# Biases as bfloat16 products in the output banks, a shorter norm chain, 60 GpSimd steps and new orders in the first and last turns of a language-model block

## The chip, the cores and the metric

The kernel runs on one core of one Trainium2 chip. The time is the device time of one launch in microseconds. PE is TensorE (its weight loads are listed as PEld), DVE is VectorE, ACT is ScalarE, POOL is GpSimd, SP is the engine that issues most of the DMAs.

## What is computed

64 sequences of 128 tokens pass through an embedding, a state-space mixer with an MLP behind it, and an 8-bit linear layer, each with a residual. Cut to what matters here:

```
h = take(quantised_table, x)                      # (64, 128, 256)
def block(x):                                     # x = layernorm(h)
    x = x + mixer(rms(x))                         # ends in  yout @ out_proj_w.T + out_proj_b
    g = gelu(rms(x) @ fc1_w.T + fc1_b)
    return x + g @ fc2_w.T + fc2_b
h = h + block(layernorm(h))
h = h + int8_linear(layernorm(h))                 # one scale from max|layernorm(h)|

mixer: z, u, B, C, dt = split(rms(x) @ in_proj_w.T); conv + silu of u, B, C
       step: z = (z + d*(u*B - A*y)) / (1 + d*d*A);  y = y + d*z;  out = y . C
       yout = (out + D_skip * u) * silu(z)
```

The biases `out_proj_b` and `fc2_b` are vectors of 256 values, the same for each token. The factor of the first norm is (var + 1e-5)^-1/2; that of the rms norm right behind it follows from the same variance.

## The kernel before

Three stages, each a block of its own. Stage 1 (to about 174 us) streams the embedding table for its maxima, gathers the 8192 rows into `h` (which stays in SBUF, tokens on partitions) and loads the weights; the last of them (`LATE_WEIGHTS`, among them both biases broadcast to 128 partitions, `out_b` and `fc2_b`) are counted on `w_late`. Stage 3 (from about 1270 us) is the 8-bit layer. Stage 2 lies between, and the change is in it.

Stage 2 takes the sequences in 16 groups of four (`G`), in turns that are software-pipelined by hand. In turn g the `first` part works on group g (input projection, convolutions, its recurrence), the `second` on group p = g-1 (scan by attention-like products, gate, output projection), the `third` on group m = g-2 (MLP), the `fourth` on group g-3 (maximum of the next norm), and `nxt` prepares the rows of group g+1. `turns` (line 1244) runs turns 0 to 3 unrolled, a loop over turns 4 to 14, and 15 to 18 unrolled; in turns 0 to 2 the later parts are missing, in turns 16 to 18 the first ones. Each engine has its own `turn` function (`pe_turn`, `act_turn`, `dve_turn`, `pool_turn`), which writes out its order; the engines meet by semaphores alone, and each executes strictly in the order written, so the order and the waits decide everything.

What the change and the prediction touch:

- `dve_quantise` (551, 554) and `dve_row_stats` (561 to 569) prepare group g+1. `pool_norm_factors` (578 to 592) makes the norm factors by a chain of nine small GpSimd operations. ACT applies them (602), PE transposes the rows (615), ACT copies them out (626), PE makes the small projections (641) and the large ones (630, 977).
- The recurrence has 64 steps of two operations. GpSimd does steps 0 to 57 (`POOL_STEPS`; 780, 782), with `pool_rms` of the group before after step 42 (`RMS_STEP`; 1117, 1119), which waits for ACT's sums of squares (1111). DVE does the last six steps (787, 789), then the keys, one reciprocal per head group (921) and the queries (927).
- PE transposes u (1001), ACT copies it to `utok` (1010), PE makes the scores of a head group (1049), DVE masks them (1060, four operations), PE makes the scan's output (1070), DVE adds the skip (1077) and gates (1084).
- `pe_out` (1095) multiplies by `w_out` into the banks `sbk`; `dve_x2` (1102) adds the layer-normed rows `xl`. Before that `dve_biases` (1025, 1027) has added `out_b` to `xl` and `fc2_b` to the rows of `h`.
- ACT sums squares (1111) and scales the rows (1128), PE transposes them (1134), ACT copies them (1141) and seeds `sbk` with the residual (1148). `pe_fc1` (1161), `act_gelu` (1171) and `pe_fc2` (1180) alternate, tile by tile, PE's down-projection three tiles behind (`LEAD`); `dve_h2` (1192) adds the banks to `h`.
- `act_x3` (1233) and `dve_max3` (1239, 1241) take the maximum of the next norm; the last group's ends stage 2.

In a full turn PE's tail of the MLP is interleaved with the scan like this (`pe_turn`, n counts tiles):

```python
for n in range(FT + LEAD):
    if third and n < FT: pe_fc1(pe, m, n, p if second else None)
    if second and n == FT:     pe_u_T(..., 0); pe_u_T(..., 1)
    if second and n == FT + 1: pe_u_T(..., 2); pe_u_T(..., 3)
    if second and n == FT + 2: pe_scores(pe, p, 0)
    if third and n >= LEAD: pe_fc2(pe, m, n - LEAD)
```

## Time and profile before

| what | value |
|---|---|
| median of 3 runs | 1327.42 us (1327.36 to 1331.47) |
| the profiled execution's own time | 1328.54 us |
| its span, first to last instruction | 1326.7 us |
| PE busy | 1124.5 us, 85% of the span |
| PE weight loads busy | 750.6 us, 57% |
| DVE busy | 1126.1 us, 85% |
| ACT busy | 791.5 us, 60% |
| POOL busy | 729.5 us, 55% |
| mean granted TensorE clock | 0.97 |

Busy time is that of instructions in execution; matmuls overlap each other's ends, so PE's counts latencies too. The granted clock is 1.00 for 2.4 GHz and 0.50 for 1.2 GHz. The profile's row of slices shows the stages: DMA at nine tenths and PE mostly below four tenths up to about 170 us, then PE at nine tenths from about 260 to 1230 us, then the last stage, in which DVE is busiest. A timeline row joins neighbouring instructions of one line on one engine: its start, its length, what it is, how many, and in brackets the idle time before it with the instruction whose end ended it.

### The profile page before, as it was taken

Reading aid. Unit: us, or ns where it says so; the run is one execution under the profiler, and the core shown is the slowest. Engines: PE = TensorE matmul, PEld = TensorE weight load, DVE = VectorE, ACT = ScalarE, POOL = GpSimd, SP = SyncE. Lnnn points to the kernel's source line nnn. Section 1 sums busy time; section 2 is a strip of 40 time slices with the busy share of each in tenths; the row PEclk is TensorE's granted clock in tenths of the full one; section 3 lists DMA queues with packets and bytes.
Section 4 is the critical chain, followed back from the end, with each engine's and each line's share of the span. In section 5 each row is a group of like instructions: output and inputs, shape, how many; then the busy total and the mean of one; then the engine's idle time right before and its main releaser. Section 6 shows DMA issues by size and latency. Waiting matters only on the chain. (4 is left out here: it accounts for less than half of the span.)

```text
span 1326.7 us, 24942 instructions
## 1 busy us (share of the span) xinstructions
PE 1124.5 (85%) x7199; PEld 750.6 (57%) x7206; DVE 1126.1 (85%) x2030; ACT 791.5 (60%) x1275; POOL 729.5 (55%) x2066
## 2 busy tenths in 40 slices
PE   2991034699999999999999999999999999997956
PEld 1550012467575766666666666576766666756534
DVE  5998969979898989898998989898989897976077
ACT  4666547383848484847475665747474848452267
POOL 8881010747485757575757575756667575730000
PEclk9999997699999999999999999999999999998879
DMA  9999801010101010101000000001010101000015
GB/s 363 407 407 419 350 11 41 1 35 2 35 1 35 1 34 1 33 4 30 10 24 15 19 18 16 18 16 28 6 34 0 34 0 35 2 18 0 0 64 190
DMA packets 37137, 91.60 MB, mean 69 GB/s; under 512 B 10141, under 2 KB 21746, under 8 KB 32738
## 3 DMA queue, kind: packets, MB, share of 16 engines
q1 hardware_dynamic: 33442, 81.32, 17.6%
q0 software_dynamic: 3072, 8.39, 1.6%
q10 hardware_dynamic: 576, 1.31, 0.3%
q8 instruction: 23, 0.38, 0.1%
q14 instruction: 24, 0.20, 0.1%
HBM read 81.29 MB, written 9.70 MB: 69 GB/s over the span
## 5 line engine op out<-in xcount | busy, mean ns | idle before, releaser
L780 POOL TENSOR_TENSOR stp<-Gs,X 128x32 f32<-128x32 f32 x870 | 263.6, 303 | 250.0 <-ACT X L753 174.9
L782 POOL TENSOR_TENSOR Gs<-Gs,stp 128x32 f32<-128x32 f32 x870 | 275.2, 316 | 68.0
L1180 PE MATMUL bank<-w_fc,gl 128*128 128x256 f32 x1024 | 244.6, 382 | 5.9 <-ACT gl L1171 5.9
L1161 PE MATMUL bank<-mT,w_fc 128*128 128x512 f32 x512 | 239.5, 601 | 1.4 <-ACT mT L1141 1.4
L1180 PEld LDWEIGHTS bank<-w_fc,gl 128*128 128x128 f32 x1024 | 189.6, 190 | 70.7 <-issue 29.7
L630 PE MATMUL bank<-xT,w_in 128*128 128x512 f32 x448 | 206.5, 601 | 0.1
L942 ACT ACTIVATE uT<-bank,cols 128x512 f32<-128x512 f32 x64 | 47.9, 774 | 229.9 <-DVE sz L1084 212.9
L1161 PEld LDWEIGHTS bank<-mT,w_fc 128*128 128x128 f32 x512 | 96.0, 192 | 87.3 <-issue 81.3
L956 DVE SCALAR_TENSOR_TENSOR uT<-bank,cols,uT 128x500 f32<-128x500 f32 (+1 forms) x192 | 133.5, 736 | 2.4
L630 PEld LDWEIGHTS bank<-xT,w_in 128*128 128x128 f32 x448 | 81.6, 191 | 83.6 <-issue 77.6
L345 DVE TENSOR_TENSOR peak<-ring,peak 128x1536 f32<-128x1536 f32 (+2 forms) x67 | 115.4, 1722 | 8.2 <-ACT ring L247 6.6
L247 ACT ACTIVATE ring<-ring 128x3072 f32<-128x3072 f32 (+4 forms) x36 | 90.8, 2531 | 49.3 <-DMA ring<-in_table 49.3
L1171 ACT ACTIVATE gl<-bank,cols 128x512 f32<-128x512 f32 x128 | 81.4, 682 | 56.9 <-PE bank L1180 49.7
L1095 PE MATMUL bank<-w_out,sz 128*128 128x256 f32 x512 | 113.9, 380 | 0.1
L1095 PEld LDWEIGHTS bank<-w_out,sz 128*128 128x128 f32 x512 | 97.3, 190 | 20.7 <-issue 7.5
L921 DVE RECIPROCAL rm<-rm 128x512 f32<-128x512 f32 x32 | 107.2, 3349 | 0.5
L753 ACT ACTIVATE X<-d_rep,cols 128x512 f32<-128x512 f32 x64 | 71.9, 1196 | 34.4 <-DMA d_rep<-d_rows 34.4
L231 POOL DMA_INDIRECT h<-in_table,ids x64 | 81.4, 1272 | 19.5 <-issue 19.2
L1060 DVE TENSOR_TENSOR MT<-bank,causal 128x512 f32<-128x512 f32 x128 | 79.3, 680 | 13.3 <-PE bank L1049 13.3
L1070 PE MATMUL bank<-MT,utok 128*64 128x128 f32 x1024 | 69.0, 286 | 24.9 <-DVE MT L1060 23.7
L1070 PEld LDWEIGHTS bank<-MT,utok 128*64 128x64 f32 x1024 | 58.1, 142 | 45.3 <-DVE MT L1060 33.0
L285 PE MATMUL bank<-ts,hot 4*128 4x256 f32 x128 | 60.4, 648 | 19.0 <-ACT hot L258 14.0
(205 smaller groups left out, 1879.2 us busy)
## 6 DMA issues: line engine op xcount, KB each, us to landing
ring<-in_table SPq DMA_DIRECT2D x31, 1536.0 KB
d_rep<-d_rows SPq DMA_DIRECT2D x128, 64.0 KB, 2.0
out<-res SPq DMA_DIRECT2D x16, 512.0 KB, 2.9
b_rep<-bc_rows SPq DMA_DIRECT2D x128, 32.0 KB, 1.8
c_rep<-bc_rows SPq DMA_DIRECT2D x128, 32.0 KB, 1.8
w_fc<-in_w_fc SPq DMA_DIRECT2D x2, 1024.0 KB, 8.5
ring<-in_table SPq DMA_DIRECT2D x2, 768.0 KB
w_in<-in_w_in ACTq DMA_DIRECT2D x1, 1088.0 KB
```

The source lines that it names most:

```text
L231: pool.indirect_dma_start(out=h[:, b * D:(b + 1) * D], out_offset=None, in_=table, in_offset=bass.IndirectOffsetOnAxis(ap=ids[:, b:b + 1], ...
L247: act.activation(ring[n % RING][0:np_, 0:nr, :], ring[n % RING][0:np_, 0:nr, :], ACT.Abs) \
L345: return dve.tensor_tensor(acc, ring[t][0:np_, r0:r0 + nr, :], acc, ALU.max)
L630: last = pe.matmul(dst, w_in[:, k, c0:c1], xT[:, k, :], start=(k == 0), stop=(k == KD - 1))
L780: pool.tensor_tensor(stp[:], Gs[:, t, ::-1, :], X2[:, t, :, :], ALU.mult).then_inc(rec.sem, 1)
L782: pool.tensor_tensor(Gs[:, t + 1, :, :], Gs[:, t, :, :], stp[:], ALU.add).then_inc(rec.sem, 1)
L921: dve.reciprocal(half_rm, half_rm).then_inc(inverted.sem, 1)
L956: dve.scalar_tensor_tensor(acc[:, :, i:], ps[:, :, 0:LEN - i], c("u_tap", f * TAPS + TAPS - 1 - i), acc[:, :, i:], ALU.mult, ALU.add).then ...
L1070: last = pe.matmul(pj[head // 2][64 * (head % 2):64 * (head % 2) + 64, j * LEN:(j + 1) * LEN], utok[:, j, head * HP:(head + 1) * HP], MT[h ...
L1095: last = pe.matmul(sbk[n][:, (j % 2) * D:(j % 2 + 1) * D], sz[:, f, j * LEN:(j + 1) * LEN], w_out[:, f, :], start=(f == 0), stop=(f == UT ...
L1161: last = pe.matmul(pj[n % 4][:, :], w_fc1[:, k, n * P:(n + 1) * P], mT[:, k, :], start=(k == 0), stop=(k == KD - 1))
L1180: last = pe.matmul(sbk[j // 2][:, (j % 2) * D:(j % 2 + 1) * D], gl[n % LEAD][:, j * LEN:(j + 1) * LEN], w_fc2[:, n, :], start=False, stop= ...
```

## The change

Four things, in stage 2.

1. **Biases on PE.** Both biases come by one DMA into `utok` (unused so far), and `dve_split_biases` makes from them a bfloat16 value, a bfloat16 remainder and a remainder of that, on partition ranges, so that three rows of `bias3` sum to the float32 value; `pick` is a 128x128 bfloat16 matrix with ones in rows 0, 64 and 96. The product `pick.T @ bias3` puts the bias on each token. `pe_bias` issues it for a whole bank (512 columns): it starts the accumulation of `pe_out`, and is added to the seeded banks ahead of the first `pe_fc2`. The DVE operations 1025 and 1027 are gone.
2. **Norm factors** by five GpSimd operations: DVE computes (1 + 1e-6) var + 1e-11 and GpSimd takes its power at once, in place of the chain of squares and products.
3. **60 GpSimd steps** in the recurrence, the rms factors after step 44, and four DVE steps.
4. **Orders.** `pe_warm` issues products whose result nobody reads: ten before turn 0, twelve in turn 1 between the transpositions, five in turn 17 ahead of the MLP's. In turn 1 DVE makes the second queries and the masks first, then quantises group 2, and takes its statistics behind the second masks. In turn 16 PE's scan pieces stand between the last down-projections, the output projection goes to the banks `tb`, ACT copies `utok` ahead of the last gelu, and DVE adds the MLP's result behind the gates. In turn 17 `act_x3` stands ahead of the gelus and `dve_max3` ahead of `dve_h2`.

```diff
-RMS_STEP = 43
-POOL_STEPS = 58
+RMS_STEP = 45
+POOL_STEPS = 60
@@ 
+        def dve_split_biases(dve):
+            whole, rest = utok[:, 0, :], utok[:, 1, :]
+            b3 = bias3[:].rearrange("p i c -> p (i c)")
+            dve.memset(pick[:], 0.0).then_inc(pick_cleared, 1)
+            dve.wait_ge(pick_cleared, 1)
+            for r in (0, 64, 96):
+                dve.memset(pick[r:r + 1, :], 1.0)
+            dve.wait_ge(bias_in, 16)
+            dve.tensor_copy(b3, whole).then_inc(halved, 1)
+            dve.wait_ge(halved, 1)
+            dve.tensor_tensor(rest[64:P], whole[64:P], b3[64:P], ALU.subtract).then_inc(halved, 1)
...
+        def pe_bias(pe, dst, i, start):
+            pe.matmul(dst[:, :].rearrange("p (j c) -> p j c", j=2), pick[:],
+                      bias3[:, i, :].unsqueeze(1).to_broadcast([P, 2, D]), start=start, stop=False,
+                      skip_group_check=True)
@@ dve_row_stats, pool_norm_factors
+            dve.tensor_scalar(lnst[:, 3, :], mv[:, :, 1], 1.0 + 1e-6, 1e-11, ALU.mult, ALU.add).then_inc(bn.sem, 1)
...
-            pool.tensor_tensor(lnst[:, 3, :], lnst[:, 2, :], lnst[:, 2, :], ALU.mult).then_inc(ln.sem, 1)
+            pool.tensor_tensor(lnst[:, 6, :], lnst[:, 3, :], half[:, 0:G], ALU.pow).then_inc(ln.sem, 1)
@@ pe_out, pe_fc2
+                pe_bias(pe, bank[n], OUT_B, True)
...
+                for i in range(2):
+                    pe_bias(pe, sbk[i], FC2_B, False)
@@ pe_turn
+        def pe_warm(pe, dst, n):
+            for _ in range(n):
+                pe.matmul(dst[:, :], ident[:], w_out[:, 0:2, :].rearrange("p f c -> p (f c)"), start=True, stop=True,
+                          skip_group_check=True)
...
+                    if last and n == FT:
+                        for j in range(G):
+                            pe_u_T(pe, p, None, j)
+                        pe_scores(pe, p, 0)
@@ dve_turn
-                if second and first and third:
-                    dve_biases(dve, p)
+                if second and not (first and third) and filling:
+                    dve_queries(dve, p, 1)
```

Where instructions moved. First PE in turn 16, from the fourth-last down-projection (1180 before, 1193 now) to the transposition of turn 17's MLP (1134, 1145). Before:

```order
L1180 MATMUL bank<-w_fc,gl 128x256 x4
L1001 MATMUL bank<-ident,uT 128x128 x8
L1180 MATMUL bank<-w_fc,gl 128x256 x4
L1001 MATMUL bank<-ident,uT 128x128 x8
L1180 MATMUL bank<-w_fc,gl 128x256 x4
L1049 MATMUL bank<-Qf,Kf 128x64 x32
L1180 MATMUL bank<-w_fc,gl 128x256 x4
L1070 MATMUL bank<-MT,utok 64x128 x16
L1049 MATMUL bank<-Qf,Kf 128x64 x32
L1070 MATMUL bank<-MT,utok 64x128 x16
L1095 MATMUL bank<-w_out,sz 128x256 x16
L1134 MATMUL bank<-ident,xr 128x128 x8
```

and now (1017 transposes u, 1057 the scores, 1078 the scan's output, 568 a bias product, 1106 the output projection, 1273 the warming products):

```order
L1193 MATMUL bank<-w_fc,gl 128x256 x4
L1017 MATMUL bank<-ident,uT 128x128 x16
L1057 MATMUL bank<-Qf,Kf 128x64 x32
L1193 MATMUL bank<-w_fc,gl 128x256 x4
L1078 MATMUL bank<-MT,utok 64x128 x16
L1057 MATMUL bank<-Qf,Kf 128x64 x32
L1193 MATMUL bank<-w_fc,gl 128x256 x4
L1078 MATMUL bank<-MT,utok 64x128 x16
L1193 MATMUL bank<-w_fc,gl 128x256 x4
L568 MATMUL bank<-bias,pick 128x512
L1106 MATMUL bank<-w_out,sz 128x256 x8
L568 MATMUL bank<-bias,pick 128x512
```

Each scan piece now has a down-projection behind it. Then DVE in turn 1, from the second reciprocal on. Before:

```order
L921 RECIPROCAL rm<-rm 128x64x8
L551 TENSOR_SCALAR h<-h,tok 128x256 x4
L554 TENSOR_SCALAR h<-h,tok 128x256 x4
L561 BN_STATS st<-h 128x6 x4
L564 BN_AGGR mv<-st 128x2 x4
L568 TENSOR_SCALAR lnst<-mv 128x4
L569 TENSOR_SCALAR lnst<-mv 128x4
L1060 TENSOR_TENSOR MT<-bank,causal 128x512 x4
L927 SCALAR_TENSOR_TENSOR Qf<-rm,Qf 128x512
L1025 TENSOR_TENSOR xl<-xl,out_b 128x1024
L1027 TENSOR_TENSOR h<-h,fc_b 128x1024
L1077 SCALAR_TENSOR_TENSOR uT<-uT,cols,bank 128x512 x2
```

and now (937 the reciprocal, 943 the query, 1068 the masks, 576 and 579 the quantising, 1085 the skip, 586 the statistics):

```order
L937 RECIPROCAL rm<-rm 128x64x8
L943 SCALAR_TENSOR_TENSOR Qf<-rm,Qf 128x512
L1068 TENSOR_TENSOR MT<-bank,causal 128x512 x4
L576 TENSOR_SCALAR h<-h,tok 128x256 x4
L579 TENSOR_SCALAR h<-h,tok 128x256 x4
L1085 SCALAR_TENSOR_TENSOR uT<-uT,cols,bank 128x512 x2
L1068 TENSOR_TENSOR MT<-bank,causal 128x512 x4
L586 BN_STATS st<-h 128x6 x4
```

The query moved ahead of the masks, quantising and statistics behind them. Last PE in a loop turn, around the first down-projection, now:

```order
L1172 MATMUL bank<-mT,w_fc 128x512 x4
L568 MATMUL bank<-bias,pick 128x512 x2
L1193 MATMUL bank<-w_fc,gl 128x256 x4
L1172 MATMUL bank<-mT,w_fc 128x512 x2
L1193 MATMUL bank<-w_fc,gl 128x256 x4
```

The two bias products stand between the up-projections (1172, before 1161) and the first down-projection; before, nothing stood there.

## Rows read from the trace of the kernel before

**Rows 1.** Stretches: us, busy (instructions) of PE, PEld, DVE, ACT, POOL; PEclk, DMA, GB/s

```profile
255.00:1207.00 952.00, 928.71 (x6284) 623.77 (x6278) 844.16 (x1568) 586.37 (x1055) 616.96 (x1921) 1.00 0.07 18
1224.40:1234.50 10.10, 7.50 (x15) 4.00 (x16) 1.18 (x7) 4.70 (x9) 1.80 (x6) 0.50 0.01 2
```

**Rows 2.** Timeline, PE, loop turn: start, us, engine, line, operation, out<-in [idle before <-releaser]

```profile
661.47 1.04 PE L1134 MATMUL bank<-ident,xr 128*128 128x128 f32 x8
667.21 3.60 PE L1161 MATMUL bank<-mT,w_fc 128*128 128x512 f32 x8
671.12 1.99 PE L1180 MATMUL bank<-w_fc,gl 128*128 128x256 f32 x8 [0.31 <-ACT gl L1171]
693.97 1.99 PE L1180 MATMUL bank<-w_fc,gl 128*128 128x256 f32 x8
697.18 2.29 PE L1070 MATMUL bank<-MT,utok 128*64 128x128 f32 x32 [1.22 <-DVE MT L1060]
...
725.11 0.60 PE L1134 MATMUL bank<-ident,xr 128*128 128x128 f32 x4
```

**Rows 3.** Instructions of L1070, what PE idled for before them: us, times

```profile
  DVE MT L1060: 23.7, 14
```

**Rows 4.** Timeline of DVE, the same loop turn

```profile
668.60 0.19 DVE L787 TENSOR_TENSOR stp<-Gs,X 128x32 f32<-128x32 f32 x1
...
693.52 1.21 DVE L1025 TENSOR_TENSOR xl<-xl,out_b 128x1024 f32<-128x1024 f32 x1
694.65 1.27 DVE L1027 TENSOR_TENSOR h<-h,fc_b 128x1024 f32 x1
695.85 2.47 DVE L1060 TENSOR_TENSOR MT<-bank,causal 128x512 f32<-128x512 f32 x4
```

**Rows 5.** Timeline of PE, one bfloat16 product of the last stage

```profile
1281.14 1.03 PE L1574 MATMUL bank<-wholeT,w_q 128*128 128x512 bf16 x4
```

**Rows 6.** Timeline of POOL, ahead of the square-root factors of a loop turn

```profile
719.47 0.22 POOL L1117 TENSOR_TENSOR ssq<-ssq,eps 128x4 f32<-128x4 f32 x1 [1.14 <-ACT gl L1111]
```

**Rows 7.** Timelines of ACT, PE and POOL, turn 0

```profile
174.57 2.19 ACT L1475 ACTIVATE w_fc<-w_fc,cols 128x1024 f32<-128x1024 f32 x2 [17.84 <-PEq L162]
...
186.23 1.94 PE L615 MATMUL bank<-ident,xr 128*128 128x128 f32 x8 [14.60 <-ACT xr L602]
188.10 2.16 PE L641 MATMUL bank<-xT,w_in 128*32 128x128 f32 x32
...
179.88 1.14 POOL L578 TENSOR_TENSOR lnst<-lnst,half 128x4 f32<-128x4 f32 x1 [74.21 <-DVE lnst L569]
183.79 0.19 POOL L592 TENSOR_TENSOR off<-lnst 128x4 f32<-128x4 f32 x1
```

**Rows 8.** Timelines of PE and DVE, turn 1

```profile
250.53 3.68 PE L1070 MATMUL bank<-MT,utok 128*64 128x128 f32 x32 [5.49 <-DVE MT L1060]
...
244.38 1.33 DVE L551 TENSOR_SCALAR h<-h,tok 128x256 f32<-128x256 f32 x4
...
249.20 2.47 DVE L1060 TENSOR_TENSOR MT<-bank,causal 128x512 f32<-128x512 f32 x4
251.59 1.00 DVE L927 SCALAR_TENSOR_TENSOR Qf<-rm,Qf 128x512 f32<-128x512 f32 x1
```

**Rows 9.** Timelines of PE and DVE, turns 16 and 17

```profile
1209.80 3.68 PE L1070 MATMUL bank<-MT,utok 128*64 128x128 f32 x32 [4.35 <-DVE MT L1060]
1213.41 8.00 PE L1095 MATMUL bank<-w_out,sz 128*128 128x256 f32 x32
1226.31 1.97 PE L1134 MATMUL bank<-ident,xr 128*128 128x128 f32 x8 [4.89 <-ACT xr L1128]
...
1260.16 1.21 DVE L1239 TENSOR_REDUCE mx<-rm 128x4 f32<-128x1024 f32 x1
```

**Rows 10.** Groups of ACT instructions: line, operation, shapes, count | busy us, mean ns | idle before

```profile
L1171 ACT ACTIVATE gl<-bank,cols 128x512 f32<-128x512 f32 x128 | 81.4, 682 | 56.9 <-PE bank L1180 49.7 <-PE bank L1161 7.0
L1010 ACT ACTIVATE utok<-bank 128x512 f32<-128x512 f32 x64 | 34.7, 594 | 21.4 <-PE bank L1001 21.4
```

More of the change, by code:

```diff
@@ L111, in build @@
         cols = sb("cols", [P, WIDTH])
[L112 to L113 removed]
+        bias3 = sb("bias3", [P, 2, D], BF16)
+        pick = sb("pick", [P, P], BF16)
         tok = sb("tok", [P, 3, SEQS])
@@ L1084, in dve_gate, with pe_out @@
                 dve.tensor_tensor(sz[:, f, :], sz[:, f, :], uT[:, f, :], ALU.mult).then_inc(yg_ready.sem, 1)
-        def pe_out(pe, g):
+        def pe_out(pe, g, bank):
             pe.wait_ge(m_ready.sem, m_ready.at(g))
-            if since(g):
+            if since(g) and bank is sbk:
                 pe.wait_ge(h2_ready.sem, h2_ready.at(g - 1))
+            if not since(g):
+                pe.wait_ge(halved, 5)
             for n in range(2):
+                pe_bias(pe, bank[n], OUT_B, True)
                 for j in (2 * n, 2 * n + 1):
@@ L1260, in turn @@
                 p, m = g - 1, g - 2
+                last = second and not first
                 for f in range(UT):
@@ L1266, in turn @@
                 if third:
+                    if not second:
+                        pe_warm(pe, pj[0], 5)
                     pe_mlp_T(pe, m)
@@ L1286, in turn @@
                         pe_ss(pe, g)
-                if second:
+                if second and first:
                     pe_scan_out(pe, p, 0, 0)
@@ L1292, in turn @@
                     pe_u(pe, g, (0, 1))
-                if second:
+                if second and first:
                     pe_scan_out(pe, p, 1, 0)
@@ L1298, in turn @@
                 if second:
-                    pe_out(pe, p)
+                    pe_out(pe, p, sbk if first else tb)
             turns(pe, turn)
@@ L1335, in turn @@
                         act_u_tap0(act, g, (2, 3))
+                if fourth and not second:
+                    act_x3(act, g - 3, GROUPS - 1)
                 for n in range(FT):
+                    if second and not first and n == FT - 1:
+                        act_utok(act, p)
                     if third:
@@ L1344, in turn @@
                         act_layer_norm(act, p)
-                if second:
+                if second and first:
                     act_utok(act, p)
-                if fourth:
-                    act_x3(act, g - 3, p if second else GROUPS - 1)
+                if fourth and second:
+                    act_x3(act, g - 3, p)
                 if first and second:
@@ L1370, in turn @@
                     dve_quantise(dve, g + 1)
+                if not second and nxt:
+                    dve_split_biases(dve)
                 if first:
@@ L1388, in turn @@
                         dve_queries(dve, p, 1)
-                if nxt and filling:
-                    dve_quantise(dve, g + 1)
-                if nxt:
+                if nxt and not filling:
                     dve_row_stats(dve, g + 1)
@@ L1403, in turn @@
                         dve_mask(dve, p, 0, hh)
-                if second and not (first and third):
+                if second and not first:
                     dve_queries(dve, p, 1)
-                    dve_biases(dve, p)
-                if third:
+                if nxt and filling:
+                    dve_quantise(dve, g + 1)
+                if first and third:
+                    dve_h2(dve, m)
+                if fourth and not second:
+                    dve_max3(dve, g - 3)
+                if third and not second:
                     dve_h2(dve, m)
@@ L1412, in turn @@
                         dve_mask(dve, p, 1, hh)
+                    if nxt and filling:
+                        dve_row_stats(dve, g + 1)
                     dve_gate(dve, p, (0, 1))
@@ L1415, in turn @@
                     dve_gate(dve, p, (2, 3))
+                if second and not first:
+                    dve_h2(dve, m)
                 if first and second:
@@ L1419, in turn @@
                 if second:
-                    dve_x2(dve, p, 0)
+                    dve_x2(dve, p, 0, sbk if first else tb)
                 if first and second:
@@ L1423, in turn @@
                 if second:
-                    dve_x2(dve, p, 1)
+                    dve_x2(dve, p, 1, sbk if first else tb)
                 if first and second:
                     dve_bc(dve, g)
-                if fourth:
+                if fourth and second:
                     dve_max3(dve, g - 3)
@@ L1457, in _ @@
             def _(sp):
+                sp.dma_start(utok[:, 0, :], a["bias"]).then_inc(bias_in, 16)
                 def turn(g, first, second, third, fourth, nxt):
@@ L1788 @@
         "w_q": wide(f["L0_ffn_weight_int8"].T).view(np.int32),
-        "out_b": rows(f["L0_attn_out_proj_b"]),
-        "fc2_b": rows(f["L0_attn_fc2_b"]),
+        "bias": rows(np.concatenate([f["L0_attn_out_proj_b"], f["L0_attn_fc2_b"]])),
         "q_cols": np.stack([tall(f["L0_ffn_weight_scale"]), tall(f["L0_ffn_bias"])], axis=1),
```

61 lines of the change are left out of this document (29 added, 32 removed).

## The prediction, made before the changed kernel had run

> **What bounds the kernel now.** I read the table of stretches first. From 255 to 1207 us, the twelve turns in which everything overlaps and their neighbours, PE is busy 928.71 of 952 us and its clock is granted in full (1.00, 2.4 GHz); DVE is busy 844 us, ACT 586, GpSimd 617 [rows 1]. The reader should see two regimes: this middle, and the first and last turns, where PE idles and then runs at 1.2 GHz (0.50 from 1224.4 to 1234.5).
>
> Then PE's timeline of one loop turn [rows 2]. From one transposition of the MLP rows (661.47) to the next (725.11) a turn takes 63.64 us, and in it PE idles twice: 0.31 us before the first down-projection (for a gelu) and 1.22 us before the scan's output products (for a mask). So 62.1 us of a turn are PE's own work, and only 1.53 us can be taken out of it by helping another engine. DVE's timeline says why PE waits 1.22 us: the scores are done about when PE begins the last down-projection (693.97), but DVE is still in the two bias additions, 1.21 and 1.27 us long, and starts the masks at 695.85 only [rows 4]. The list of what PE idled for before line 1070 has 14 waits, 23.7 us: 5.49 in turn 1 [rows 8], 4.35 in turn 16 [rows 9], and 13.9 in twelve others [rows 3].
>
> The last reading is the two ends: turn 0 and 1 [rows 7, 8], turns 16 and 17 [rows 9].
>
> A page of the Trainium skill speaks against reading PE as the bound: Trainium Kernel Development and Optimization, Performance Expectations, calls matmul busy time a bad metric and points to the weight loads' share, which here is 623.77 of 952 us, 66%. I return to it as a rival.
>
> **Part 1, biases on PE, loop turns.** Removed: two DVE additions, 2.48 us. Added: four bfloat16 products of 512 columns per turn (two ahead of the output projection, two ahead of the first down-projection). Four such products in a row took 1.03 us [rows 5]; the last one's tail overlaps, so the spacing is about 0.21 us and a turn gets 0.85 us of PE work. A 512-column float32 pass is spaced (3.60-0.59)/7 = 0.43 us, taking 0.59 for the last one's own length [rows 2]: the upper bound per product. The lower bound is zero, if they fell into idle time. I take 0.21, the same shape and type. On the same product TensorE: Matmul & The Clock Gate, Back-to-back issue gap, gives 131 ns per product of 512 columns in a real stream; with it the 64 products of the kernel would be an estimated 5 us cheaper. Rows 5 do not show it.
> The two products ahead of the down-projection (0.43 us) need only the seeded banks, so they run while PE waits its 0.31 us for the gelu. The 1.22 us go: without the additions and with two DVE steps fewer, DVE is free before the scores are; two masks of 0.62 us (2.47 for four), which the first scan products wait for, are then done before PE ends its last down-projection. So a loop turn becomes 63.64 - 0.31 - 1.22 + 0.85 = 62.96, that is -0.68. Eleven loop turns (4 to 14): **-7.5**. Turn 2 is about even; turns 3 and 15 have no mask wait to win and pay the output pair, 0.43 each, while the other pair falls into the gelu wait as in the loop: **+0.8** together.
>
> **Part 2, 60 GpSimd steps, rms factors after step 44.** A step that DVE does is two operations of 0.19 to 0.22 us [rows 4], so DVE gains 0.9 us per turn, where it has slack: no term. A GpSimd step costs 0.66 us (two of 0.33). Before the rms factors GpSimd idles 1.14 us for ACT's sums [rows 6]; two more steps ahead of them are 1.3 us, and the shorter norm factors give 1.3 back. After them 15 steps stay, as before. **0**. If that cover went, DVE's own steps would start up to 1.3 us late, end 0.4 late, with some 0.8 us before PE asks for the queries.
>
> **Part 3, norm factors.** From 179.88 to 183.98 nine GpSimd operations run in a chain [rows 7]; five remain, two powers of 1.0 to 1.1 us and three of 0.2: 2.8 us, with one more DVE operation of 0.1. 1.3 us, on the path in turn 0 only; in other turns covered by ACT's order.
>
> **Part 4, turn 0.** Ten warming products start with the stage, at about 174.6 [rows 7]. Each is two passes, 0.85 us at full clock and 1.7 at half. In turn 1 the clock rose 4.3 us after PE began at 250.5 (full from 255 [rows 1, 8]); in turn 17 8.2 us after 1226.3. With 5 us at half, the ten end at 185.8, about a microsecond after the rows are ready (184.9 instead of 186.2). The transpositions (1.94) and small products (2.16) then run at full clock, where the former take 1.04 [rows 2, 7]: the small products end near 188.4, not 190.26. **-1.8**, and everything in turn 0 hangs on them. If the clock comes at 8 us: 0. The bias splitting on DVE, some nine operations, about 3 us, lies behind DVE's quantising, while DVE would wait for those small products. Its load is issued as the stage begins, 13 us before DVE is needed again; the trace has no row for it, so I bound its delay by 0 and 1 us and take 0.
>
> **Part 5, turn 1.** DVE's block of quantising and statistics (244.38 to 249.20) moves behind the masks, one query of 1.00 us moves ahead of them [rows 8]: masks start 3.8 us earlier, and so do the scan products. The quantising (2.7) then stands ahead of the skip and the statistics ahead of the gates, but the additions (2.5) are gone: at the gates DVE is 3.2 earlier. Minus the output pair (0.43) and half a microsecond, because PE idles 3 us ahead of the masks and may lose its clock again: **-2.3** (bounds -1 and -3.4). The twelve warming products (12 us) end about 1.5 us after PE is next asked for; at full clock scores take 2.0 instead of 3.7, so nobody waits.
>
> **Part 6, turns 16 to 18.** In turn 16 the 4.35 us wait goes, since transpositions, scores and scan products now stand between the last down-projections, and the slow stretch behind it: scan and output products took 11.6 us (1209.80 to 1221.41), of which 2.0 and 7.1 are needed at full clock (32 passes each, of 128 and of 256 columns, the latter 0.215 apart, plus a tail), 2.5 less. To pay: PE idles 1.3 us for a tile copy and the last gelu, which now stands behind the copies (0.59 + 0.68 [rows 10]; the scores wait for all gelus), 0.6 for masks and gates, 0.85 for products. 4.35 + 2.5 - 2.75: **-4.1**. In turn 17 five warming products fill the 4.89 us before 1226.31; the clock stays full instead of half for 8.2 us less 0.9 of gaps, half of which is 3.7; minus 0.43 for products: **-3.3**. The maximum reduction at 1260.16 (1.21 + 0.16) moves under the down-projections: **-1.4**. Bounds: -4 and -11.
>
> **Sum**: -7.5 + 0.8 - 1.8 - 2.3 - 4.1 - 3.3 - 1.4 = -19.6. The profiled execution took 1328.54 us (span 1326.7), giving 1308.9; it lies 1.1 above the median of 1327.42, so I forecast **1307.8 us**, own range 1302 to 1313.
>
> **Rivals.**
> - *The ends give half.* The clock rises 8 us after the first product in turn 0 as it did at 1226.3, drops in turn 1 and once more in turn 16, whose waits were pieced together by hand. For it: both rise times stand in rows. Against: turn 16 has no idle above 1.5 us. 13 us shrink to 6.5: 1314. Chance 0.12.
> - *Products at the float32 rate*, 0.43 instead of 0.21, 64 times: +13.8, 1321.6. Against: rows 5. 0.08.
> - *Products cost nothing*, PE not being the bound, as the skill page's rule on busy time would have it. Then a loop turn keeps the full -1.53 (0.85 more, eleven times) and the rest pays nothing (3): 12 us lower, 1296. Against: in rows 2 groups of passes follow at exactly 0.43 us per pass. 0.04.
> - *Slower: each bfloat16 product empties the array.* It stands between float32 groups; if neither its weights nor the next ones load under a running product, each costs its full 0.39 us (1.03 - 3 x 0.21) plus the tails on both sides (0.38 - 0.21 each, by the length of a 256-column pass), 0.65 to 0.7. 64 x 0.44 = +28: 1336. It decides from 0.52 us per product, where 64 x 0.31 eats the 19.6. The last stage mixes both types and shows 0.21 inside groups, but never a lone product. 0.05.
> - *The change does not do what it says*: the masks still come late since DVE waits for something else. PE's turn would then be 64.2, +6.2 + 7.5: 1321. Rows 4 show DVE back to back up to the masks, so 0.01.
> - The forecast: 0.70.
>
> A measurement of this kernel can tell 0.3%, 4 us. Faster by more than that is below 1323.4: forecast, half ends, free products and nearly all of the float32 case, 0.90; within 0.3%: 0.05; slower: 0.05. The range 1302 to 1318 holds the forecast, the weaker ends and the product bounds up to 0.37 us; it leaves out 0.17.
>
> **What would show it.** Loop turns of 62.9 to 63.0 us from transposition to transposition; no DVE release ahead of the scan products there; bfloat16 products 0.21 apart ahead of both projections; the gelu wait gone. Small products of turn 0 ending before 189, granted clock 1.00 from about 180. Turn 17's transposition near 1211 with the clock at 1.00 until the last down-projection. Wrong: turns of 63.6 or more, 1.2 GHz stretches in turns 1 or 17, or a new wait of the scores for DVE's queries because GpSimd's 60th step came late.

## The result and the profile after

The changed kernel takes 1308.05 us (median of 4 runs, 1304.88 to 1309.22), the kernel before 1327.69 us beside it (4 runs, 1327.36 to 1331.47): a ratio of 0.9843, with a 95% interval from 0.9823 to 0.9864. That is 19.6 us less, the sum of the prediction, but two of its terms are wrong by about 4 and 5 us, in opposite directions. The profiled execution took 1309.22 us; its span is 1307.3.

The page of the changed kernel shows less busy time on DVE (1126.1 before) and POOL (729.5) and more on PE (1124.5), of whose 32 us more the warming products make 26.6 (10.93, 11.20 and 4.45 in PE's timeline):

```profile
PE 1156.5 (88%) x7317; PEld 764.9 (59%) x7324; DVE 1083.3 (83%) x1963; ACT 791.4 (61%) x1275; POOL 698.2 (53%) x2062
```

PE's timeline of a loop turn, which answers to [rows 2]:

```profile
654.21 1.04 PE L1145 MATMUL bank<-ident,xr 128*128 128x128 f32 x8
...
663.38 0.59 PE L568 MATMUL bank<-bias,pick 128*128 128x512 bf16 x2
663.87 1.99 PE L1193 MATMUL bank<-w_fc,gl 128*128 128x256 f32 x8
...
686.71 1.99 PE L1193 MATMUL bank<-w_fc,gl 128*128 128x256 f32 x8
688.64 1.97 PE L1078 MATMUL bank<-MT,utok 128*64 128x128 f32 x32
...
701.59 0.38 PE L568 MATMUL bank<-bias,pick 128*128 128x512 bf16 x1
701.81 3.62 PE L1106 MATMUL bank<-w_out,sz 128*128 128x256 f32 x16
...
716.67 0.60 PE L1145 MATMUL bank<-ident,xr 128*128 128x128 f32 x4
```

A turn takes 62.46 us (654.21 to 716.67), 1.18 less than before; 62.96 was predicted. No row has an idle time any more. The first down-projection starts 9.66 us into the turn, as before (9.65), though two bias products now stand ahead of it. The 32 scan products take 1.97 us; in [rows 2] they took 2.29, so PE had waited inside that group too. DVE's timeline of the same turn says who waits now (compare [rows 4], where DVE went straight from the additions into the masks):

```profile
685.27 0.16 DVE L595 TENSOR_SCALAR lnst<-mv 128x4 f32<-128x4 f32 x1
686.95 2.48 DVE L1068 TENSOR_TENSOR MT<-bank,causal 128x512 f32<-128x512 f32 x4 [1.52 <-PE bank L1057]
```

DVE idles 1.52 us for the scores. Turns 0 and 1 on PE, which answer to [rows 7, 8]:

```profile
175.82 10.93 PE L1273 MATMUL bank<-w_out,ident 128*128 128x512 f32 x20 [2.94 <-PEq L163]
186.59 1.04 PE L631 MATMUL bank<-ident,xr 128*128 128x128 f32 x8
187.87 1.35 PE L657 MATMUL bank<-xT,w_in 128*32 128x128 f32 x32 [0.25 <-ACT xT L642]
...
240.34 2.01 PE L1057 MATMUL bank<-Qf,Kf 32*128 32x64 f32 x64 [0.74 <-ACT utok L1026]
245.67 3.68 PE L1078 MATMUL bank<-MT,utok 128*64 128x128 f32 x32 [3.32 <-DVE MT L1068]
249.28 3.69 PE L1057 MATMUL bank<-Qf,Kf 32*128 32x64 f32 x64
```

and turns 16 and 17, which answer to [rows 9]:

```profile
1179.75 1.14 PE L1017 MATMUL bank<-ident,uT 128*128 128x128 f32 x8 [0.33 <-ACT utok L1026]
1182.39 2.65 PE L1057 MATMUL bank<-Qf,Kf 32*128 32x64 f32 x64 [1.50 <-ACT gl L1182]
1184.97 3.78 PE L1193 MATMUL bank<-w_fc,gl 128*128 128x256 f32 x8
1188.68 2.79 PE L1078 MATMUL bank<-MT,utok 128*64 128x128 f32 x32
...
1206.49 4.45 PE L1273 MATMUL bank<-w_out,ident 128*128 128x512 f32 x10
1211.55 1.09 PE L1145 MATMUL bank<-ident,xr 128*128 128x128 f32 x8 [0.60 <-ACT xr L1139]
```

The big waits of [rows 8, 9] are gone (5.49 and 4.35 us), but in both turns a smaller one is left (3.32; 0.33 and 1.50), and what stands behind it takes up to twice its length. The stretches of the changed kernel show why (columns as in [rows 1]):

```profile
244.00:250.00 6.00, 4.33 (x48) 4.00 (x48) 6.00 (x15) 0.00 (x0) 4.67 (x18) 0.58 0.01 3
250.00:255.00 5.00, 5.00 (x59) 3.85 (x58) 2.67 (x6) 0.00 (x0) 3.83 (x16) 0.50 0.00 0
1184.00:1190.00 6.00, 6.00 (x40) 4.69 (x38) 3.41 (x5) 1.47 (x3) 0.00 (x0) 0.50 0.01 3
```

The granted clock fell to 0.50 (1.2 GHz) at both waits, at 244.9 us inside the first and at 1183.6 us, 1.2 us behind the second. In turn 17 it stays at 2.4 GHz, as predicted: the first down-projections start 9.24 us after the transposition (1220.79 - 1211.55), 12.36 before (1238.67 in the trace of before, less 1226.31).

The table cuts each trace at the first MLP transposition of each turn; "turns 0, 1" begins with ACT's first scaling of the weights (174.57 before, 175.79 after). "Low clock" is how long the granted clock was at 0.50 in the later part of turn 1 (from 235 us) and in turn 16, to the nearest microsecond. The kernel before took 1327.7 us beside the changed one and 1328.2 to 1329.7 us (medians) beside the others, so a difference of 2 us between two rows of the last column is not clear of noise. The 95% interval of the ratio to the kernel before lies apart from that of the changed kernel for bias_twice, split, best and best58 alone; for the others the traces say where a difference lies.

| kernel | turns 0, 1 | low clock | loop turn | turn 16 | low clock | median of the runs (range), us |
|---|---|---|---|---|---|---|
| before | 105.6 | 20 | 63.63 | 58.2 | 7 | 1327.7 (1327.4 to 1331.5) |
| changed | 102.7 | 10 | 62.46 | 57.9 | 7 | 1308.1 (1304.9 to 1309.2) |
| no_bias | 109.3 | 28 | 62.02 | 54.5 | 10 | 1305.7 (1304.3 to 1308.7) |
| bias_twice | 104.1 | 17 | 63.17 | 58.7 | 7 | 1318.3 (1316.3 to 1319.8) |
| no_warm | 104.8 | 23 | 62.45 | 57.8 | 7 | 1311.4 (1309.6 to 1313.4) |
| dve_bias | 103.0 | 17 | 62.73 | 56.1 | 3 | 1309.2 (1308.0 to 1310.5) |
| steps58 | 100.6 | 3 | 62.46 | 57.8 | 7 | 1307.0 (1306.0 to 1308.3) |
| norm9 | 103.0 | 7 | 62.46 | 56.2 | 3 | 1306.9 (1305.9 to 1308.7) |
| old_t1 | 108.1 | 17 | 62.46 | 54.6 | 0 | 1310.4 (1310.2 to 1314.0) |
| old_t16 | 101.5 | 3 | 62.46 | 56.3 | 3 | 1304.7 (1304.4 to 1305.0) |
| fill | 100.2 | 0 | 62.47 | 54.8 | 0 | 1303.4 (1300.9 to 1306.0) |
| split | 102.9 | 7 | 62.03 | 54.8 | 0 | 1297.4 (1296.0 to 1298.5) |
| best | 100.2 | 0 | 62.02 | 54.8 | 0 | 1296.0 (1295.5 to 1297.0) |
| best58 | 99.8 | 0 | 62.49 | 54.8 | 0 | 1301.3 (1300.7 to 1303.1) |

### The profile page after: what moved, and what is told of

Its sections match the earlier page's. It is cut to its first block and busy times, and to the rows that moved or that the text cites. A ratio compares the mean times of both kernels' runs of the same rounds, so it can differ in the third digit from the quotient of the medians.

```text
span 1307.3 us, 25029 instructions
## 1 busy us (share of the span) xinstructions
PE 1156.5 (88%) x7317; PEld 764.9 (59%) x7324; DVE 1083.3 (83%) x1963; ACT 791.4 (61%) x1275; POOL 698.2 (53%) x2062
## 5 line engine op out<-in xcount | busy, mean ns | idle before, releaser
L796 POOL TENSOR_TENSOR stp<-Gs,X 128x32 f32<-128x32 f32 x900 | 260.8, 290 | 254.5 <-ACT X L769 176.2
L798 POOL TENSOR_TENSOR Gs<-Gs,stp 128x32 f32<-128x32 f32 x900 | 257.9, 287 | 70.4
L1172 PE MATMUL bank<-mT,w_fc 128*128 128x512 f32 x512 | 236.7, 595 | 1.5 <-ACT mT L1152 1.5
L1106 PEld LDWEIGHTS bank<-w_out,sz 128*128 128x128 f32 x512 | 97.3, 190 | 19.4 <-issue 5.0
L232 POOL DMA_INDIRECT h<-in_table,ids x64 | 82.2, 1285 | 19.4 <-issue 19.4
L1057 PE MATMUL bank<-Qf,Kf 32*128 32x64 f32 x2048 | 66.7, 279 | 2.2 <-ACT gl L1182 1.5
```

The source lines that it names most:

```text
L232: pool.indirect_dma_start(out=h[:, b * D:(b + 1) * D], out_offset=None, in_=table, in_offset=bass.IndirectOffsetOnAxis(ap=ids[:, b:b + 1], ...
L796: pool.tensor_tensor(stp[:], Gs[:, t, ::-1, :], X2[:, t, :, :], ALU.mult).then_inc(rec.sem, 1)
L798: pool.tensor_tensor(Gs[:, t + 1, :, :], Gs[:, t, :, :], stp[:], ALU.add).then_inc(rec.sem, 1)
L1106: last = pe.matmul(bank[n][:, (j % 2) * D:(j % 2 + 1) * D], sz[:, f, j * LEN:(j + 1) * LEN], w_out[:, f, :], start=False, stop=(f == UT - ...
L1172: last = pe.matmul(pj[n % 4][:, :], w_fc1[:, k, n * P:(n + 1) * P], mT[:, k, :], start=(k == 0), stop=(k == KD - 1))
```

## The experiments

### What the late masks cost: no_bias

```diff
-                if second and first and third:
-                    dve_biases(dve, p)
...
-                    dve_biases(dve, p)
```

> The kernel before, with the two DVE bias additions of every group left out (the output lacks both biases), nothing else changed. Theory: the late masks cost a loop turn more than the 1.22 us of idle time shown before the scan's output products; PE also waits inside that group for the third and fourth mask (the group took 2.29 us, against 1.96 when the masks are there) and loses the 0.07 us by which it would overlap. Then a loop turn falls by 1.6 us, from 63.64 to 62.0. Rival (the prediction's own term): only the 1.22 us go, 62.4 us. Rival: the masks are as late as before, 63.6. The whole kernel: 16 to 21 us below 1327.5, the larger figure if turns 1 and 16 profit too.

A loop turn took 62.02 us and the kernel 1305.7. Without the additions the scan products are one unbroken group right behind the down-projection, and only the wait for the gelu is left:

```profile
667.49 1.99 PE L1180 MATMUL bank<-w_fc,gl 128*128 128x256 f32 x8 [0.32 <-ACT gl L1171]
...
690.33 1.99 PE L1180 MATMUL bank<-w_fc,gl 128*128 128x256 f32 x8
692.26 1.97 PE L1070 MATMUL bank<-MT,utok 128*64 128x128 f32 x32
```

So the late masks had cost 1.61 us per turn: 1.22 shown as idle, 0.32 inside the group (2.29 against 1.97) and 0.07 of overlap with the group ahead. The prediction counted the first part alone. Turn 16 fell from 58.2 to 54.5 us with its old order, even with 10 us at low clock. At the other end turns 0 and 1 took 3.7 us more: in turn 1 the clock stayed at 1.2 GHz until 263 us in this trace, until 255 in that of before, with the same order of work on PE. That this is chance is inferred; the profiled execution was the slowest of the four (1308.7 us) and had the lowest mean clock (0.972, the others 0.974).

### What a product costs: bias_twice

```diff
+          for _ in range(2):
             pe.matmul(dst[:, :].rearrange("p (j c) -> p j c", j=2), pick[:],
```

> The changed kernel with each of its 64 bias products issued twice (fc2's bias then counts twice in the output). Theory: a product costs its spacing of 0.22 to 0.25 us wherever PE is busy: a loop turn of 62.46 us becomes 63.3 to 63.4, the kernel 13 to 14 us slower (1321 to 1322). Rival (free products, PE not being the bound): no change, 1308. Rival (a float32 pass's rate of 0.43): 64.2 us per turn, 1335. Rival (each empties the array, 0.65 and more): the first of a pair already did, so the second would show only its spacing; the length from the first product to the pass behind it tells that apart.

Turns of 63.17 us and 1318.3 us for the kernel: 0.71 us for four more products, and 10.3 us in all where 13 to 14 were expected. Four in a row stand 0.86 us ahead of what follows, 0.215 each:

```profile
667.74 1.03 PE L569 MATMUL bank<-bias,pick 128*128 128x512 bf16 x4
668.60 1.24 PE L1194 MATMUL bank<-w_fc,gl 128*128 128x256 f32 x5
```

The 0.15 us missing from 0.86 is at the down-projection, which in the changed kernel still waits a little for its gelu behind the pair: 0.06 us ahead of the group (663.87 - 663.38 - 0.43) and 0.10 inside it (it is 1.99 us long, 1.89 where its inputs are ready). The figure expected, 63.3 to 63.4, overlooked that. The rivals of free products (62.46) and of the float32 rate (64.2) both fall, and so does that of an emptied array: in the changed kernel, too, the lone product at 701.59 is 0.22 us ahead of the group behind it. The 131 ns of the Trainium skill's section on the back-to-back issue gap (TensorE: Matmul & The Clock Gate) appears in no run; each shows 0.21 to 0.22. The section Performance Expectations of the Trainium skill (Trainium Kernel Development and Optimization) calls matmul busy time a bad metric for how close a kernel is to roofline. That distance was not measured here. The rival of free products read it to mean that PE is not the bound of this loop; but products added to PE lengthen the turn.

### Biases back on DVE, all else kept: dve_bias

```diff
-                pe_bias(pe, bank[n], OUT_B, True)
...
-                for i in range(2):
-                    pe_bias(pe, sbk[i], FC2_B, False)
...
+                if second and first and third:
+                    dve_biases(dve, p)
```

> The changed kernel with both biases added by DVE again, where the kernel before did it, and no bias product; the 60 steps, the short norm chain, the orders and the warming products stay. Theory: in the changed kernel DVE waits 1.6 us for the scores ahead of the masks; with 2.48 us of additions it is 0.9 us late, so a loop turn is 62.02 (both waits gone but the gelu's, as measured without any bias) plus 0.9, 62.9 us: 0.44 above the changed kernel, 0.7 below the kernel before, and that 0.7 is what the two DVE steps given to GpSimd are worth. The kernel: about 1313. Rival: the 60 steps are worth nothing, the turn is 63.6 us as before, 1320. Rival: products cost so much that DVE additions are no worse, 62.4 us.

Loop turns of 62.73 us and 1309.2 us. The masks start late again, but less, and PE idles 0.34 us and waits inside the group:

```profile
687.72 2.47 DVE L1079 TENSOR_TENSOR MT<-bank,causal 128x512 f32<-128x512 f32 x4
```

```profile
689.05 2.29 PE L1089 MATMUL bank<-MT,utok 128*64 128x128 f32 x32 [0.34 <-DVE MT L1079]
```

So with the 60 steps and the short norm chain in place, moving both biases to PE brings 0.27 us per loop turn, not 1.18. (62.9 us and about 1313 were expected.)

### 58 steps, all else kept: steps58

```diff
-RMS_STEP = 45
-POOL_STEPS = 60
+RMS_STEP = 43
+POOL_STEPS = 58
```

> The changed kernel with 58 GpSimd steps (square-root factors after step 42) and six DVE steps again. Theory: DVE's slack ahead of the masks shrinks from 1.6 to 0.7 us and stays above zero, so with the biases on PE the 60 steps are worth nothing: loop turns 62.46, the kernel within 1.5 us of the changed one, 1308. Rival (the steps matter too): masks late by some tenths, 62.7 to 63.0 us per turn, 1311 to 1314.

Loop turns of 62.46 us and 1307.0 us, no difference from the changed kernel. DVE still waits for the scores:

```profile
684.67 2.48 DVE L1068 TENSOR_TENSOR MT<-bank,causal 128x512 f32<-128x512 f32 x4 [0.54 <-PE bank L1057]
```

Part 1 and part 2 relieve the same wait: without both a turn is 63.63, with the steps but not the products 62.73, with the products but not the steps 62.46, with both 62.46. All but the first have the short norm chain too; no run has the 60 steps and DVE's additions with the old chain, so the 0.90 us of dve_bias belong to the steps and the chain together.

### The warming products: no_warm

```diff
-                    if not second:
-                        pe_warm(pe, pj[0], 5)
...
-                        if not third:
-                            pe_warm(pe, sbk[0], 12)
...
-                pe_warm(pe, pj[0], 10)
```

> The changed kernel without any warming product (no 10 ahead of turn 0, no 12 in turn 1, no 5 in turn 17). Theory: turn 17 starts at half clock again and loses 3.5 us up to the end of its down-projections; turn 0's transpositions and small products take 1.94 and 2.16 us instead of 1.04 and 1.35 but start 0.3 us earlier, 1.2 us lost; turn 1 loses almost nothing (0 to 1), since its clock falls before the masks with or without them and its scores, 1.7 us longer, stand before a wait for DVE that was 3.3 us. Together 4.7 to 5.7 us slower than the changed kernel: about 1313. Rival: the products in turn 1 are worth their 2 us too, 1316. Rival: the warming is worth nothing since it delays what follows, 1308.

1311.4 us, 3.3 above the changed kernel, less than the 4.7 expected at least. From turn 17's transposition to its last down-projection 33.8 us passed instead of 30.1, so the five products of turn 17 are worth 3.7 us. Turns 0 and 1 took 2.1 us more in the one trace. The other 2.5 us do not show in the medians; the changed kernel's own four runs spread over 4.3 us, so the figure read from turn 17 is the firm one.

### The old norm chain: norm9

```diff
-        ln = signal("ln", 5)
+        ln = signal("ln", 9)
...
+            pool.wait_ge(ln.sem, ln.at(g, 1))
+            pool.tensor_tensor(lnst[:, 3, :], lnst[:, 2, :], lnst[:, 2, :], ALU.mult).then_inc(ln.sem, 1)
```

> The changed kernel with the norm factors by the old chain of nine GpSimd operations. Theory: the chain ends 1.3 us later in turn 0, where all else hangs on it; the ten warming products end 0.6 us after the rows are ready in the changed kernel, so 0.6 of the 1.3 us are not seen there: turns 0 and 1 grow by 0.7 us (plus or minus what the clock in turn 1 does), nothing changes in loop turns (62.45 us), the kernel 0.5 to 1 us slower, 1308.8. Rival: GpSimd's 60th step now comes 1.3 us later in each loop turn, and DVE's queries and masks with it; slack is 1.6 us, so if that is less than it looks, turns of 62.5 to 63.2, up to 1316.

1306.9 us: in the total it can't be told from the changed kernel. Loop turns are 62.46, so GpSimd's cover holds. In turn 0 the small products ended 1.6 us later after the start of the stage than in the changed kernel (its PE row at 188.32 is 1.35 long and the stage starts at 174.59, so 15.1, against 189.22 - 175.79 = 13.4). That is more than the 0.7 expected, because the chain itself was longer than before:

```profile
183.24 0.33 POOL L613 TENSOR_TENSOR lnst<-lnst 128x4 f32<-128x4 f32 x1
183.64 0.65 POOL L615 TENSOR_TENSOR lnst<-lnst 128x4 f32<-128x4 f32 x1
184.24 0.18 POOL L616 COPY rs<-lnst 128x4 f32<-128x4 f32 x1
184.39 0.36 POOL L617 TENSOR_TENSOR off<-lnst 128x4 f32<-128x4 f32 x1
```

In the kernel before the same four took 0.20, 0.20, 0.18 and 0.19 us. Beside them DVE now splits the biases:

```profile
183.08 0.43 DVE L557 CAST bias<-utok 128x512 bf16<-128x512 f32 x1
183.54 0.69 DVE L559 TENSOR_TENSOR utok<-utok,bias 64x512 f32<-64x512 f32 x1
```

The short chain is over (183.92) before the first of DVE's two subtractions starts (184.82), and does not meet it.

### Turn 1 in its old order: old_t1

```diff
+                if nxt and filling:
+                    dve_quantise(dve, g + 1)
+                if nxt:
                     dve_row_stats(dve, g + 1)
...
-                if second and not (first and third) and filling:
-                    dve_queries(dve, p, 1)
```

> The changed kernel with DVE's order of turn 1 as before (quantising and statistics of group 2 ahead of the masks, the second queries behind them); the twelve warming products stay. Theory: the masks start 3.8 to 4.9 us later, PE idles 8 us ahead of the scan products, and its clock falls in every execution, while in the changed kernel it falls for a length that differs between executions; turns 0 and 1 take 105 to 107 us against 100.6 to 102.9 in the traces with the new order, the kernel 2 to 4 us more than the changed one, 1310 to 1312. Rival: the order is worth nothing, since DVE does the same work up to the gates either way and only PE's clock counts, 1308.

1310.4 us, 2.4 above the changed kernel, and 108.1 us for turns 0 and 1. PE idles 6.84 us ahead of the scan products, and 17 us of low clock follow:

```profile
248.59 3.68 PE L1078 MATMUL bank<-MT,utok 128*64 128x128 f32 x32 [6.84 <-DVE MT L1068]
252.20 3.69 PE L1057 MATMUL bank<-Qf,Kf 32*128 32x64 f32 x64
255.82 6.39 PE L646 MATMUL bank<-xT,w_in 128*128 128x512 f32 x8
```

In the trace turns 0 and 1 are 5.4 us longer than in the changed kernel; turn 16, which kept its full clock in this execution, is 3.3 us shorter. So the sign is shown and the size is not: 2.4 us by the medians, 5.4 by the traces, where the prediction had bounds of 1 and 3.4. (105 to 107 us were expected for turns 0 and 1.)

### Turn 16 in its old order: old_t16

```diff
-                    if last and n == FT:
-                        for j in range(G):
-                            pe_u_T(pe, p, None, j)
-                        pe_scores(pe, p, 0)
...
-                    pe_out(pe, p, sbk if first else tb)
+                    pe_out(pe, p, sbk)
```

> The changed kernel with turn 16 in its old order on PE, ACT and DVE (down-projections first, output projection into the same banks as ever); turns 1 and 17 keep theirs. Theory: what turn 16 lost before was mostly the two additions (their 2.5 us stand ahead of the masks of the second head group there); without any bias the old order took 54.5 us, so with bias products it takes 55.0 to 55.5, against 57.85 in the changed kernel, whose new order idles 1.8 us ahead of the scores and loses the full clock: 2 to 3 us faster, 1305.5. Rival (the prediction's): the new order is what removes the 4.35 us wait, the old one gives 60 us, 1310. Both within a few us, so the length of turn 16 in the trace decides, from transposition to transposition.

1304.7 us, faster than the changed kernel by 3.4, of which the trace puts 1.5 in turn 16 (56.3 us instead of 57.9); the remainder lies in turns 0 and 1 and between executions. The old order waits 2.08 us for the masks of the second head group where it had waited 4.35 [rows 9], and its scan products run at low clock for 3 us:

```profile
1191.17 3.44 PE L1078 MATMUL bank<-MT,utok 128*64 128x128 f32 x32 [2.08 <-DVE MT L1068]
```

So over half of the 4.35 us went with the two additions: no_bias, which differs from the kernel before in them alone, waits 2.08 us there too. The new order brings no gain as long as the clock falls in it. (55.0 to 55.5 was expected of the old one, without low clock.) Nor need it bring any at full clock: the slow scan products cost 1.5 us here (3.44 against 1.97), so by estimate the old order would take 54.8 us, as long as fill (below) takes with the new one. No run has the old order with bias products at full clock.

### More warming: fill

```diff
                             pe_u_T(pe, p, None, j)
+                        pe_warm(pe, pj[0], 2)
                         pe_scores(pe, p, 0)
...
                         pe_scores(pe, p, 0)
+                        if not third:
+                            pe_warm(pe, sbk[0], 4)
```

> The changed kernel with six more warming products: four in turn 1 behind the first scores, where PE idled 3.32 us for the masks, and two in turn 16 ahead of the first scores, where it idled 1.50 us for the last gelu. Theory: the clock that fell to 1.2 GHz in both places (245 to 255 us and 1184 to 1191 us) stays full; the work under it gets back 2.5 to 3 us in turn 1 (scan products 3.68 to 2.0, scores 3.69 to 2.0, DVE's second masks that much earlier) and 3.3 us in turn 16 (2.65, 3.78 and 2.79 us to 2.0, 2.0 and 1.96), less 0.1 to 0.3 us by which the products overrun the waits: 5 to 6 us faster than the changed kernel, about 1302.5. Rival: DVE sets the pace in turn 1 whatever PE's clock, only turn 16 gains, 1305. Rival: the clock falls all the same, and the kernel is unchanged or 0.5 us slower, 1308.5.

1303.4 us, 4.6 below the changed kernel. In its trace the clock stays full in both places:

```profile
244.00:250.00 6.00, 5.80 (x101) 4.22 (x100) 6.00 (x15) 0.00 (x0) 4.65 (x18) 1.00 0.01 3
250.00:255.00 5.00, 4.80 (x39) 2.68 (x37) 4.80 (x16) 0.00 (x0) 3.92 (x14) 1.00 0.00 0
1176.00:1184.00 8.00, 8.00 (x110) 6.14 (x112) 5.19 (x6) 2.04 (x4) 0.00 (x0) 1.00 0.01 2
1184.00:1190.00 6.00, 5.92 (x111) 5.12 (x108) 4.97 (x9) 2.08 (x4) 0.00 (x0) 1.00 0.01 3
```

Turns 0 and 1 fell by 2.5 us, turn 16 by 3.1 to 54.8. Over all traces with the new turn 16 its length follows the low clock in it: 57.8 to 58.7 with 7 us, 56.1 and 56.2 with 3, 54.6 to 54.8 with none. (One of these, old_t1, kept the full clock without any product more: the fall is likely there, not certain.) The runs of fill still spread over 5 us, and its trace is of the fastest (1300.9 us, mean clock 0.988); the two slowest had 0.985, so in these the clock must have been low for some 8 us more, and the six products do not hold it in every execution.

### Each bias where it costs nothing: split, best and best58

```diff
-                pe_bias(pe, bank[n], OUT_B, True)
+                if biased:
+                    pe_bias(pe, bank[n], OUT_B, True)
...
+                if second and first and third:
+                    dve_out_bias(dve, p)
```

> The kernel with six more warming products, and the output projection's bias given back to DVE in turns 2 to 15 (one addition of 1.21 us ahead of the masks); the down-projection's bias stays on PE, as does the other in turns 1 and 16. Theory: the pair ahead of the down-projection lies in the wait for the gelu and costs nothing, the pair ahead of the output projection costs 0.43 us, and DVE has 1.6 us of slack ahead of the masks: a loop turn of 62.47 becomes 62.03 to 62.1 us, 14 turns give 6 us, 1297.5 against 1303.4. Rival: the addition makes the masks late again (slack used up by the wait for its operands), 62.5 to 63 us per turn, 1303 to 1310.

1297.4 us, loop turns of 62.03, the length that no_bias has without any bias. DVE's addition fits into its wait, of which 0.37 us are left:

```profile
681.23 1.21 DVE L1043 TENSOR_TENSOR xl<-xl,out_b 128x1024 f32<-128x1024 f32 x1
682.81 0.69 DVE L1075 TENSOR_TENSOR MT<-bank,causal 128x512 f32<-128x512 f32 x1 [0.37 <-PE bank L1064]
```

In its trace the clock fell at 240 us in turn 1, though fill had kept it there; hence one step more:

```diff
-                            pe_warm(pe, sbk[0], 12)
+                            pe_warm(pe, sbk[0], 13)
...
+                        if not third:
+                            pe_warm(pe, sbk[0], 1)
                         pe_scores(pe, p, 0)
...
-                pe_warm(pe, pj[0], 10)
+                pe_warm(pe, pj[0], 9)
```

> The kernel with the output bias on DVE in turns 2 to 15 and the extra warming products, with three counts changed: 9 warming products instead of 10 ahead of turn 0 (they ended 0.6 us late), 13 instead of 12 in turn 1 and one more ahead of the first scores there, to close waits of 0.5 to 1.0 us that stood where the clock fell at 240 us. Theory: turns 0 and 1 take 99.5 to 100.5 us instead of the 102.9 of that kernel's trace, the rest is as it was: about 1295, and the spread between executions shrinks. Rival: the clock falls there all the same, 1297.4.

1296.0 us (5 runs, 1295.5 to 1297.0): 0.9756 of the kernel before, interval 0.9742 to 0.9769, and 12 us below the changed kernel. Turns 0 and 1 take 100.2 us, and the runs spread over 1.5 us, with mean clocks of 0.987 to 0.989. The last run took the two GpSimd steps away from it (the diff is that of steps58):

> The last version (output bias on DVE in turns 2 to 15, 9, 13, 1, 4, 2 and 5 warming products) with 58 GpSimd steps and six DVE steps. Theory: the steps and the biases relieve DVE of the same wait, so what one is worth depends on the other: with both biases on PE the two steps were worth nothing (slack 1.52 us before, 0.54 us after taking them back), with the output bias on DVE only 0.37 us of slack is left, and 0.9 us more work makes the masks 0.5 us late: loop turns of 62.3 to 62.6 us against 62.02, the kernel 3 to 6 us slower, about 1300.5. Rival (no effect, as before): 62.02 and 1296.0.

1301.3 us and loop turns of 62.49. With only 0.37 us of DVE slack left, the same two steps that were worth nothing in the changed kernel are worth 0.47 us per turn.

## Why the prediction was right in sum and wrong in two terms

The trace after less that of before gives -19.4 us of span. The profiled execution began stage 2 1.2 us later (175.79 against 174.57), in a stage that the change hardly touches; of the twelve experiments' traces ten begin it between 174.2 and 175.4 and two at 175.8 or 175.9, so this is put down to the execution. The rest, by the prediction's own steps:

| step | predicted | trace | judged |
|---|---|---|---|
| loop turns, 11 | -7.5 | -12.9 | mis-sized |
| turns 2, 3 and 15 | +0.8 | +0.2 | about right |
| turns 0 and 1 | -4.1 | -2.9 | turn 0 right, turn 1 lost to a low clock |
| turn 16 | -4.1 | -0.3 | wrong |
| turn 17 to the last down-projection | -3.3 | -3.1 | right |
| maximum moved, and stage 3 | -1.4 | -1.5 | right |

**Loop turns.** The step that failed is "63.64 - 0.31 - 1.22 + 0.85". The price of a product was right (0.21 predicted, 0.215 measured). Two sizes were off. The mask wait was worth 1.61, not 1.22, since it went on inside the group of scan products, where [rows 2] show it only as 2.29 us for 32 products. And the pair ahead of the down-projection was charged 0.43 against a wait of 0.31, a net cost of 0.12; it costs nothing (no_bias and split, without and with the pair, both have turns of 62.02 to 62.03). The wait for the gelu was larger than the 0.31 us shown as well: PE also lost the 0.16 us by which a group overlaps the one ahead (667.21 + 3.60 - 0.16 is where the next would have begun) and 0.10 inside the down-projection (1.99 in [rows 2]). The pair's 0.43 fits into these 0.57. 62.02 + 0.43 for the pair at the output projection is the 62.46 measured.

**The step counts as no term.** Part 2 said 0, and that is so beside the products (steps58). But the prediction booked the whole mask wait under Part 1 and named the two steps there only in passing, where dve_bias and steps58 show two sets of edits that each remove over half or all of it, and best58 that their worth depends on what else DVE carries.

**Turn 16.** "Turn 16 has no idle above 1.5 us" was the argument for a full clock. The idle of 1.50 us, behind one of 0.33, was enough: the clock fell, and the scores, a down-projection and the scan products took 9.2 us (2.65 + 3.78 + 2.79) where fill needs 6.0. These 3.2 us are the gap between predicted and measured but for half a microsecond. The rival "the ends give half" named this place; it priced it with 6.5 us, and turn 17 and the end did not share in it.

**Turns 0 and 1.** The clock rose at 180.1 us, 4.3 us after the first warming product (5 were assumed, 8 by the rival), and the small products ended 13.4 us after the start of the stage, 15.7 before: -2.3 where -1.8 was predicted. The masks of turn 1 then came 3.8 us earlier still, as predicted (they start 68.6 us into the stage, 74.6 before). But the gates, where 3.2 us were to be left, came only 0.1 us earlier than turn 0 had made them, since DVE now had to wait for scores that PE made at 1.2 GHz:

```profile
253.04 2.48 DVE L1068 TENSOR_TENSOR MT<-bank,causal 128x512 f32<-128x512 f32 x4 [2.33 <-PE bank L1057]
```

So turn 1 lost all but 0.6 us of its 2.3 to 10 us of low clock, of which the forecast allowed half a microsecond's worth. Steps58 and old_t16, with the same order of work in turn 1, had 3 us of it and stand at -5.0 and -4.1. How much of that belongs to the kernel and how much to the execution is open. The spread of the changed kernel's own four runs is not explained by the clock: the profiled one, the slowest (1309.2 us), had the highest mean clock of the four (0.983), the fastest (1304.9 us) 0.982.

So the right total rests partly on errors that cancel, and that is luck. The prediction gives two ranges, 1302 to 1313 with the sum and 1302 to 1318 behind the rivals; both held because they reached both ways.

## What to carry to other kernels

A wait costs more than the idle time ahead of a group: look for the group's own length at another place where its inputs are ready, and add the overlap that an idle engine loses. When two edits relieve the same wait, take each back alone before keeping both; here the best version came from giving each bias to the engine that was waiting at that point. Where a matrix engine must idle for 1 to 3 us at a full clock, as PE did here, check the granted clock behind it, and look at several executions before crediting an order with the result.

## What the runs showed of the hardware that was not expected

- The granted clock fell behind waits as short as 0.33 and 1.50 us in turn 16, in six of the seven traces with that order and no product in the wait, and the length of a low stretch differed between traces with the same order of work on PE: in turn 1 it was 3 to 17 us in six traces with the changed kernel's order (changed, bias_twice, dve_bias, steps58, norm9, old_t16), 20 and 28 us in two with the old one (before, no_bias). Each is one execution of a kernel that differs elsewhere. In bias_twice, dve_bias and split it fell at 240 us already, behind waits of 1.0 to 1.6 and of 0.7 us.
- A bfloat16 product of 512 columns between float32 groups costs just its 0.215 us; its weight load takes 98 ns, the float32 ones of the projections 190 to 192 and those of the transpositions 141 to 143:

```profile
L568 PEld LDWEIGHTS bank<-bias,pick x64: 97/98/98, 263.0 to 1220.4; 128*128 128x128 bf16 x64
```

- Three GpSimd operations on 4 elements per partition took 0.33 to 0.65 us instead of 0.19 to 0.20 beside DVE's float32 copies and subtractions (norm9). That DVE held GpSimd up is inferred from the times; no run separated the two.
